# Edge messages summed in windows of 64 destinations instead of 128, in a graph layer with attention and experts

## What is computed

```python
xn = layernorm(x)
# graph part: a message per edge, picked by relation and source, summed per destination
all_msg = einsum('nf,rfo->rno', xn, weight)            # 16 relations
gate    = sigmoid(einsum('nf,rf->rn', xn, gate_weight))
msg     = all_msg[rel_type, src] * norm * gate[rel_type, src][:, None]
agg     = relu(segment_sum(msg, dst, num_segments=6250))
# linear attention over all nodes, 8 heads: k^T v summed over the nodes, then q times it
x = x + agg + mix(xn)
# 8 experts with gelu, the best 2 of each node weighed by a softmax
x = x + moe(layernorm(x))
```

## Time and profile before

| | |
|---|---|
| runs before | median 1955.37 us of 3 (1952.18 to 1957.35) |
| profiled execution | 1947.87 us, its span 1946.0 us |
| PE busy | 95% of the span, granted clock 0.982 on average |
| PEld (weight loads) busy | 81% |
| DVE, ACT, POOL busy | 59%, 41%, 40% |

### The profile page before, as it was taken

The page is one execution under the profiler, slowest core; times in us unless marked ns, Lnnn a source line. Parts: engine busy times, 40 slices in busy tenths (PEclk is TensorE's granted clock), DMA queues, the critical chain, the costliest instruction groups (busy, mean ns, idle before and its releaser), DMA issues.

```text
span 1946.0 us, 28360 instructions
## 1 busy us (share of the span) xinstructions
PE 1852.5 (95%) x10189; PEld 1574.4 (81%) x10189; DVE 1152.4 (59%) x3290; ACT 803.9 (41%) x1454; POOL 769.8 (40%) x812
## 2 busy tenths in 40 slices
PE   5999999999997699998799999999999999999998
PEld 4878888888886599998688888888888887888987
DVE  6564555444443577777566767666676675766753
ACT  4555555555553333331133334333343343433443
POOL 2000000000000467667766666556566566556500
PEclk8999999999999799999899999999999999999999
DMA  7665777655552664444333343333434334233300
GB/s 215 227 230 212 282 292 286 227 224 222 214 203 118 250 233 142 155 132 154 106 112 104 105 125 93 114 98 109 122 88 124 102 101 133 67 117 108 96 17 16
DMA packets 113868, 295.55 MB, mean 152 GB/s; under 512 B 18106, under 2 KB 73778, under 8 KB 104406
## 3 DMA queue, kind: packets, MB, share of 16 engines
q1 hardware_dynamic: 75200, 189.27, 26.5%
q0 software_dynamic: 38528, 104.46, 18.5%
HBM read 162.70 MB, written 130.96 MB: 151 GB/s over the span
## 4 chain that ended last, share of the span: by engine, by line
PE 83%; DVE 6%; ACT 3%; DMA 3%; POOL 2%; issue 2%; SPq 1%; DVEq 0%; ACTq 0%
PE bank L51 21%; PE bank L53 19%; PE bank L52 19%; PE bank L1325 15%; POOL plain L582 2%; PE bank L1314 2%; PE bank L1424 2%; DMA messages<-plain 2%; DVE parts L612 1%; DVE plain L967 1%; PE bank L1371 1%; ACT parts L1148 1%; PE bank L1218 1%; DVE plain L801 1%; PE bank L1438 1%
## 5 line engine op out<-in xcount | busy, mean ns | idle before, releaser
L582 POOL DMA_INDIRECT plain<-messages,idxT x784 | 759.0, 968 | 1066.5 <-issue 873.4
L51 PE MATMUL bank<-parts 128*128 128x512 f32 (+1 forms) x1864 | 756.9, 406 | 29.4 <-DMA parts<-xnT_scratch 22.1
L53 PE MATMUL bank<-parts 128*128 128x512 f32 (+1 forms) x1864 | 722.1, 387 | 0.0
L52 PE MATMUL bank<-parts 128*128 128x512 f32 (+1 forms) x1864 | 719.9, 386 | 0.0
L51 PEld LDWEIGHTS bank<-parts 128*128 128x128 f32 x1864 | 353.3, 190 | 116.9 <-issue 34.5
L1325 PE MATMUL bank<-plain 128*128 128x128 f32 x3136 | 389.7, 279 | 24.3 <-DMA plain<-messages,idxT 18.9
L53 PEld LDWEIGHTS bank<-parts 128*128 128x128 f32 x1864 | 352.1, 189 | 70.6
L1325 PEld LDWEIGHTS bank<-plain 128*128 128x128 f32 x3136 | 378.1, 195 | 33.4 <-DMA plain<-messages,idxT 21.3
L52 PEld LDWEIGHTS bank<-parts 128*128 128x128 f32 x1864 | 353.9, 190 | 56.3
L1148 ACT CAST parts<-plain 128x512 fp32r<-128x512 f32 (+1 forms) x208 | 123.8, 595 | 396.9 <-DVE plain L967 396.9
L612 DVE TENSOR_TENSOR parts<-plain,parts 128x512 fp32r<-128x512 f32 (+2 forms) x242 | 161.9, 672 | 209.4 <-ACT parts L1148 143.2
(11 more groups left out here) (153 smaller groups left out, 1095.7 us busy)
## 6 DMA issues: line engine op xcount, KB each, us to landing
messages<-plain SPq DMA_DIRECT2D x48, 2048.0 KB, 6.8
parts<-xnT_scratch SPq DMA_DIRECT2D x20, 1024.0 KB, 5.3
xnT_scratch<-parts SPq DMA_DIRECT2D x98, 128.0 KB, 3.3
plain<-messages,idxT POOLq DMA_INDIRECT x784, 2.8
w_parts<-parts SPq DMA_DIRECT2D x32, 256.0 KB, 2.4
parts<-w_parts SPq DMA_DIRECT2D x4, 2048.0 KB, 20.1
plain<-in_x SPq DMA_DIRECT2D x48, 128.0 KB, 7.1
plain<-in_x SPq DMA_DIRECT2D x10, 512.0 KB, 4.3
```

The lines of the kernel that those rows point to most:

```text
L51: e.matmul(out, left(0), right(0), start=start, stop=False)
L52: e.matmul(out, left(0), right(1), start=False, stop=False)
L53: return e.matmul(out, left(1), right(0), start=False, stop=stop)
L582: e.indirect_dma_start(msg[:, b % SLOTS, j, :], None, table_rows, bass.IndirectOffsetOnAxis(idxT[:, j, b:b + 1], 0)).then_inc(s_gather[b % ...
```

## The change

`WINDOW` goes from 128 to 64. So a one-hot matrix has 64 columns instead of 128, the moving operand of each of the 8 matmuls of a batch has 64 columns, their results take 128 columns of the bank instead of 256, and the addition into `agg` is 128 columns wide instead of 256. The stationary operands, the number of instructions on each engine, their order and their waits are the same. The guard now asks for a range below 64. The general path keeps its width of 128 in the same memory (`onehot_all`).

```diff
-WINDOW = P
+WINDOW = P // 2
...
-    AGG = TILES * P + WINDOW
+    AGG = TILES * P + P
...
         onehot = plain.carve(HOTS, CHUNKS, WINDOW)
+        plain.at += HOTS * CHUNKS * (P - WINDOW)
+        onehot_all = onehot.rearrange("p a b c -> p (a b c)")[:, 0:CHUNKS * P].rearrange("p (j n) -> p j n", j=CHUNKS)
...
                 for j in range(CHUNKS):
-                    m = e.tensor_scalar(onehot[:, b % HOTS, j, :], iota[:, :], offT[:, j, b:b + 1], nrmT[:, j, b:b + 1],
+                    m = e.tensor_scalar(onehot[:, b % HOTS, j, :], iota[:, 0:WINDOW], offT[:, j, b:b + 1], nrmT[:, j, b:b + 1],
                                         ALU.is_equal, ALU.mult)
...
-                        basei[0:1, b:b + n], engines=[e.engine], min_val=0, max_val=AGG - WINDOW,
+                        basei[0:1, b:b + n], engines=[e.engine], min_val=0, max_val=AGG - P,
...
                 cols = agg[:, :, bass.ds(base[b], WINDOW)]
-                e.tensor_tensor(cols, cols, bank[b % 2][:, 0:D].rearrange("p (h n) -> p h n", h=KH), ALU.add).then_inc(s_add_batch, 1)
+                e.tensor_tensor(cols, cols, bank[b % 2][:, 0:KH * WINDOW].rearrange("p (h n) -> p h n", h=KH), ALU.add).then_inc(s_add_batch, 1)
...
-                                    o = e.tensor_scalar(onehot[:, 0, j, :], iota[:, :], dstG[:, j:j + 1], nrmG[:, j:j + 1],
+                                    o = e.tensor_scalar(onehot_all[:, j, :], iota[:, :], dstG[:, j:j + 1], nrmG[:, j:j + 1],
...
-                        m = e.matmul(bank[b % 2][:, h * P:(h + 1) * P], msg[:, b % SLOTS, j, h * P:(h + 1) * P],
+                        m = e.matmul(bank[b % 2][:, h * WINDOW:(h + 1) * WINDOW], msg[:, b % SLOTS, j, h * P:(h + 1) * P],
                                      onehot[:, b % HOTS, j, :], start=j == 0, stop=j == CHUNKS - 1)
...
                                         m = e.matmul(bank[0][:, h * P:(h + 1) * P], msg[:, 0, j, h * P:(h + 1) * P],
-                                                     onehot[:, 0, j, :], start=j == 0, stop=j == CHUNKS - 1)
+                                                     onehot_all[:, j, :], start=j == 0, stop=j == CHUNKS - 1)
```

## The result

The changed kernel takes 1959.47 us (median of 20 runs, 1955.91 to 1966.03), the kernel before 1954.49 us in its 20 runs (1948.46 to 1957.75). The ratio is 1.0027, with a 95% interval of 1.0018 to 1.0036: about 5 us slower, by less than the 0.3% that I had called no change, but clear of its own uncertainty and in the other direction than forecast. The two profiled executions lie further apart, 11 us, since that of the kernel before (1947.87 us) was faster than each of its 20 runs; the size of the effect is read from the medians.

The account below looks back on a forecast made before the run. PE's own pace, set in batch sums by weight loads, was taken as the bound. Batch sums 0 and DVE 1.5 us saved gave 1954 us against the median of 1955.4; range 1944 to 1964 us, no change 75%.

Parts of the forecast that it names:

- What bounds the kernel: Whole kernel: PE's own pace decides; in batch sums the 128 by 128 weight load sets it, 0.112 us between records.
- Batch sums cost 0: 3136 batch-sum records on PE: distance stays 0.112 us with 64 columns; forecast 0 us, bounds 0 and 176 us.
- Rival A: Batch sums on PE: the moving side paces them after all; 176 us gained, about 1790 us; chance 4%.
- DVE's relief: One-hots and additions on DVE: 45 us less busy time, 0.3 to 9 us of it on the path, 1.5 taken.
- Gathers unchanged: Gathers on POOL: same number, size and slots, 0.946 us each; PE's 18.9 us of waits for them stay.
- Rival C: PE's batches: thinner sums lower the clock; 1.6 us per half-clock batch, burst stretch 2 or 3 us; slower, chance 9%.
- Its sign: Granted clock between 1000 and 1850 us: stays at 1.00; under 0.99 would show the falling clock at work.
- The other sign: Busy times in the changed kernel's trace: PE's stays within 10 us while DVE's falls by 30 to 60 us.
- The sum: Whole kernel: 0 for batch sums, 1.5 us saved through DVE; profiled execution 1947.9 to 1946.4 us, median 1954 us.

## Why the prediction was wrong

- **What bounds the kernel**: right. PE's pace decides, and it is the pace of the weight loads. Sixteen records of 64 columns span 1.89 us in a full-clock batch, those of 48 columns 1.88, those of 128 columns 1.95. Only the last record of a batch got shorter, 0.217 us against 0.270 by the shortest records of the earlier trace rows and of the changed kernel, which is more than the 0.01 us that I gave it and still nothing on the path. The loads still last 0.192 us. Rival A is out.
- **Batch sums cost 0**: here it failed. The step priced the 3136 records by their own distance and stopped there; the clock was left to a rival and stood in the sum at nothing. The distance did stay; what the term left out is that the columns which a batch passes also bear on the clock of the wide matmuls behind it. Measured by the version with only the matmuls narrow, the term is +9.2 us (1.0047) and not 0.
- **DVE's relief**: the mechanism was right, its size too small. 45 us of busy time were forecast and 50 came (addition 0.289 us, one-hot 0.333). On the path it is worth 3.5 us (0.9982), against 1.5 taken; it lies in the range of 0.3 to 9.
- **Gathers unchanged**: their number and length were; PE's waits for them fell from 18.9 to 9.7 us in the profiled executions, so they did not stay, as the text had it. But that is a slower PE arriving later, not a gain.
- **Rival C** had the mechanism, but only 9%. Its 2 or 3 us for the burst stretch fit the 2.7 us (0 to 5) measured there. For the rest it looked at batches that are themselves at half clock, 1.6 us each, and at long runs of batches: these hold their clock with 64 columns and lose it with 48. What it missed is the third stretch, where most of the loss is in the experts' matmuls after the batch. Its sign, a clock under 0.99 from 1000 to 1850 us, was set just too low: the row shows 0.99 with 23.4 us at half clock in it. The other sign, that PE's busy time stays within 10 us, failed: it rose by 21. And the row that I set against it, sixteen 16-column matmuls at full pace to their end, was no evidence: in the changed kernel too such a run is at full pace to its end, and the drop comes one batch later. What would have told more is the pair of rows router and batch read together: the kernel before already lays the batch right behind the router's narrow matmuls, and the change halves the columns of the batch.
- **The sum**: -1.5 us forecast; 9.2 - 3.5 = +5.7 us by the two halves, +5.3 measured (1.0027, of 1954 us). The time itself, 1959.5 us, lies inside the range of 1944 to 1964 us; the direction doesn't.

The Trainium skill, "TensorE: Matmul & The Clock Gate", section "HAM oscillation — how this bites in real kernels", lays drops of the clock to gaps in which PE is idle. The start of the long drop at 926.8 us fits that, since PE is then in a wait of 4.67 us for a gather. Its length doesn't: PE's later waits in it are 0.23 to 1.34 us. In the version with only the matmuls wide they are longer there, 0.68 to 2.96 us, and yet the clock comes back after 3.4 or 6.8 us each time. The drop at 1199.8 us doesn't fit either, since PE has no gap from 1191.7 us up to it.

Left open: why only four of the nine places with a router and a batch drop (with only the matmuls narrow it is four as well, but two of them others), what brings the drop at 1644 us, what exactly is counted, and what the chip with the pauses has. The change itself was not measured on that chip.

## What to carry to other kernels

Narrowing a matmul whose pace its weight load sets gains nothing on TensorE, and can cost: work that passes few columns may lower the granted clock, and the bill is paid by whatever wide matmul comes next. So when a change takes columns away, look at which narrow runs already stand side by side, keep them apart with wide ones, or leave the columns in (here as zeros) and narrow only the other engines' share: that version, at 0.9982, beats both kernels, by 0.2% and 0.5%. In a profile, compare the granted clock by stretches before asking who waits for whom.

## What the runs showed of the hardware that I had not expected

The granted clock fell to half while PE issued matmuls without a gap: after 16 matmuls of 16 columns and a batch of 64 columns (1199.8 us, changed kernel), and within four batches of 48 columns (1735.9 us). With 128 columns in the same batches the same places held full clock, and so did four batches of 64 columns with no router before them (1722.3 us, changed kernel). The ratio to the kernel before goes with the columns: 0.9982 at 128 (VectorE at 64), 1.0004 at 96, 1.0027 at 64, 1.0107 at 48 (VectorE as wide as the matmuls), while the distance from record to record stays at 0.112 us at full clock. Once down, the clock also stayed down for 47.6 us (926.8 us) with batches of 64 columns, where it came back after 3.4 or 6.8 us with 128.
